# Output projection of the few-key cross-attention: one full-precision product against three rounded products

## The reference

```python
x = layernorm(x + attn(x))                       # a polynomial block and a gated feed-forward (1248 wide)
x = layernorm(x + xattn(x, ctx, mask))           # 32 heads of width 128
x = layernorm(x + ffn(x))                        # gated feed-forward (1376 wide)

# xattn
h_q, h_k, h_v = heads(rmsnorm(x) @ w_q.T), heads(ctx @ w_k.T), heads(ctx @ w_v.T)
score = softmax(where(mask, einsum('bqhd,bkhd->bhqk', h_q, h_k) + position_bias, -inf))
attn  = einsum('bhqk,bkhd->bqhd', where(mask, score, 0), h_v)
return x + attn.reshape(b, lq, 32 * 128) @ w_out.T
```

## Time and profile before

| | before |
|---|---|
| median of 3 runs | 782.0 us (781.49 to 782.08) |
| the profiled execution, its own time | 782.88 us |
| its span, first to last instruction | 781.1 us |
| PE busy | 738.4 us (95%) |
| DVE busy | 486.3 us (62%) |
| ACT busy | 402.5 us (52%) |
| POOL busy | 91.6 us (12%) |
| mean granted TensorE clock | 0.993 of full speed |
| head loop | about 223 to 640 us of the span |

### The profile page before, as it was taken

One profiled execution on the slowest core, in us unless ns is written; L12 is line 12 of the kernel. 1 busy time (PEld: TensorE's weight loads), 2 busy tenths in 40 slices (PEclk: granted clock), 3 DMA queues, 4 the chain that ended last, 5 costly groups with the idle time before them and its releaser, 6 DMA issues.

```text
span 781.1 us, 12357 instructions
## 1 busy us (share of the span) xinstructions
PE 738.4 (95%) x4320; PEld 582.0 (75%) x4320; DVE 486.3 (62%) x823; ACT 402.5 (52%) x617; POOL 91.6 (12%) x86
## 2 busy tenths in 40 slices
PE   6999999999988999999999999999999878998994
PEld 4888888888867777777777777777777547886883
DVE  5653467534352688777886586665566647578655
ACT  5433333333345666655676666766666444554452
POOL 2010000090017000000000031000000001304503
PEclk9999999999999999999999999999999999999998
DMA  9353241332625788888886777766765323542641
GB/s 331 117 219 136 84 145 54 108 122 81 241 83 179 247 300 288 265 272 290 278 277 210 227 240 232 226 222 225 245 220 175 106 96 110 155 141 84 214 133 54
DMA packets 60039, 145.09 MB, mean 186 GB/s; under 512 B 6752, under 2 KB 6768, under 8 KB 59344
## 3 DMA queue, kind: packets, MB, share of 16 engines
q1 hardware_dynamic: 58400, 136.73, 53.8%
q0 software_dynamic: 1360, 7.23, 2.4%
q10 hardware_dynamic: 224, 0.39, 0.2%
HBM read 142.23 MB, written 2.10 MB: 185 GB/s over the span
## 4 chain that ended last, share of the span: by engine, by line
PE 82%; DVE 11%; issue 2%; ACT 2%; DMA 2%; POOL 1%; DVEq 0%; ACTq 0%; POOLq 0%
PE bank L468 25%; PE acc L468 16%; PE bank L640 7%; PE bank L586 7%; PE acc L721 7%; PE bank L699 6%; PE bank L682 5%; PE bank L605 5%; DVE score L1319 2%; DVE prob L1347 1%; DVE row_sum L1341 1%; DVE piece_top L1335 1%; DVE neg_max L1325 1%; PE bank L500 1%; PE bank L666 1%
## 5 line engine op out<-in xcount | busy, mean ns | idle before, releaser
L468 PE MATMUL bank<-feat_hi,a_hi 128*128 128x512 f32 x352 | 139.3, 396 | 11.0 <-DVE feat_lo L1102 7.5
L468 PE MATMUL bank<-feat_lo,a_hi 128*128 128x512 f32 x352 | 138.0, 392 | 0.0
L1102 DVE TENSOR_TENSOR a_lo<-a_raw,a_hi 128x1024 fp32r<-128x1024 f32 (+1 forms) x45 | 55.4, 1232 | 124.3 <-ACT a_hi L867 118.0
L996 ACT ACTIVATE t_ring<-bank 128x512 f32<-128x512 f32 x64 | 70.1, 1095 | 86.3 <-PE bank L605 86.3
L586 PEld LDWEIGHTS bank<-few_ctx,ak 128*128 128x128 f32 x512 | 62.8, 193 | 45.1 <-issue 42.4
L468 PE MATMUL acc<-b_hi,tile_hi 128*128 128x512 f32 x224 | 87.7, 392 | 3.6 <-issue 1.9
L1341 DVE TENSOR_REDUCE row_sum<-prob 128x4 f32<-128x512 f32 x64 | 43.7, 683 | 71.3 <-ACT prob L1011 70.9
L468 PEld LDWEIGHTS bank<-feat_hi,a_hi 128*128 128x128 f32 x352 | 66.8, 190 | 28.0 <-DVE a_lo L1102 9.6
L468 PE MATMUL acc<-b_hi,tile_lo 128*128 128x512 f32 x224 | 87.2, 389 | 0.0
L605 PEld LDWEIGHTS bank<-k_ring,wq 128*128 128x128 f32 x512 | 64.5, 192 | 18.7 <-issue 13.4
L586 PE MATMUL bank<-few_ctx,ak 128*128 128x128 f32 x512 | 74.4, 289 | 3.4 <-DMA ak<-ax 2.1
(11 more groups left out here) (113 smaller groups left out, 1097.4 us busy)
## 6 DMA issues: line engine op xcount, KB each, us to landing
ak<-ax SPq DMA_DIRECT2D x64, 512.0 KB, 3.8
wq<-wqn SPq DMA_DIRECT2D x64, 256.0 KB, 4.2
wv<-wvh SPq DMA_DIRECT2D x64, 256.0 KB, 3.4
wo<-bx SPq DMA_DIRECT2D x64, 256.0 KB, 4.0
a_raw<-w SPq DMA_DIRECT2D x22, 512.0 KB, 4.1
a_raw<-a SPq DMA_DIRECT2D x21, 512.0 KB, 3.7
b_raw<-b SPq DMA_DIRECT2D x34, 256.0 KB, 2.7
pair<-w SPq DMA_DIRECT2D x24, 352.0 KB, 4.4
```

What stands on the lines that cost most here:

```text
L468: mm = pe.matmul(out_ap, w, x, start=start and k == 0, stop=stop and k == len(products) - 1, skip_group_check=True)
L996: act.activation(t_ring[n // GH % 2][:].rearrange("p c b k h -> p (c b k h)")[:, n % GH:GH * N:GH], bank[0][:], ACT.Copy).then_inc(t_ok, 1)
L1102: return dve.tensor_tensor(out_ap, whole, high, ALU.subtract)
```

## The change

`outer(n)` becomes three rounded products by `passes`. The operands are made as follows.

- ACT: `round_wo(n-1)` in step n, between `copy_turned` and `exponentials`, rounds the weight `wo` (128x512) into `wo_hi`. It waits for the weight's load, for the matmul that last read this `wo_hi` buffer, and for POOL's last use of it.
- POOL: `wo_rest(n)` computes `wo_lo` = `wo` - `wo_hi` (128x512), one per head. The layer norms of POOL are cut into pieces that stand between these subtractions (`normalise(1)` over heads 0 to 7, `normalise(2)` over heads 36 to 40), and the scan's `partition_all_reduce` stands behind the one of head 30.
- DVE: `split_values(n-1)` after `divide(n-1)` makes `v_hi` (a 128x128 copy) and `v_lo` (a 128x128 subtraction).
- PE: `outer(n)` waits for `v_lo_ok` and `wo_lo_ok` in place of `wo_dma`. SP's `load_o(n)` and ACT's `copy_values(n)` get one more wait each.

The new tiles lie in buffers that are free in the head loop (`tile_hi`, `tile_lo`, `b_hi`, `b_lo` of the feed-forward blocks).

```diff
+        wo_hi, wo_lo = tile_hi, tile_lo
+        v_hi, v_lo = [b_hi[i][:, 0:P] for i in range(2)], [b_lo[i][:, 0:P] for i in range(2)]
...
                 if n >= 2:
                     sp.wait_ge(out_used, n - 1)
+                    sp.wait_ge(wo_lo_ok, n - 1)
                 sp.dma_start(wo[n % 2][:], bx[n % HEADS]).then_inc(wo_dma[n % 2], 16)
...
+            def wo_rest(n):
+
+                pool.wait_ge(wo_hi_ok, n + 1)
+                pool.tensor_tensor(wo_lo[n % 2][:], wo[n % 2][:], wo_hi[n % 2][:].bitcast(F32),
+                                   ALU.subtract).then_inc(wo_lo_ok, 1)
...
             pool.wait_ge(xn_ok, C)
-            normalise(1)
-
-            pool.wait_ge(top_ok, 1)
-            pool.partition_all_reduce(piece_all[:, 1:2], piece_all[:, 0:1], P, bass.bass_isa.ReduceOp.max).then_inc(all_ok, 1)
-            pool.wait_ge(all_ok, 1)
-            pool.tensor_copy(low_flag[:], piece_all[:, 1:2]).then_inc(flag_ok, 1)
-            normalise(2)
+            scales(1)
+            for n in range(HN):
+                if n < TT:
+                    centre(1, n)
+                elif n < 2 * TT:
+                    level(1, n - TT)
+                wo_rest(n)
+                if n == GH + SCANS + 2:
+                    pool.wait_ge(top_ok, 1)
+                    pool.partition_all_reduce(piece_all[:, 1:2], piece_all[:, 0:1], P, bass.bass_isa.ReduceOp.max).then_inc(all_ok, 1)
+                    pool.wait_ge(all_ok, 1)
+                    pool.tensor_copy(low_flag[:], piece_all[:, 1:2]).then_inc(flag_ok, 1)
+                if n == HEADS + 4:
+                    scales(2)
+                if HEADS + 4 < n <= HEADS + 4 + TT:
+                    centre(2, n - HEADS - 5)
...
                     if few:
-                        pe.wait_ge(wo_dma[par], 16 * (n // 2 + 1))
-                        mm = pe.matmul(bank[1][:], v_sb[par][:, 0:P], wo[par][:], start=True, stop=True)
+                        pe.wait_ge(v_lo_ok, n + 1)
+                        pe.wait_ge(wo_lo_ok, n + 1)
+                        mm = passes(bank[1][:], v_hi[par], v_lo[par], wo_hi[par][:], wo_lo[par][:], True, True)
...
+            def round_wo(n):
+
+                act.wait_ge(wo_dma[n % 2], 16 * (n // 2 + 1))
+                if n >= 2:
+                    act.wait_ge(u_mm, n - 1)
+                    act.wait_ge(wo_lo_ok, n - 1)
+                else:
+                    act.wait_ge(b_used, T30)
+                act.activation(wo_hi[n % 2][:], wo[n % 2][:], ACT.Copy).then_inc(wo_hi_ok, 1)
...
                 if n >= 1:
                     copy_turned(n - 1)
+                    round_wo(n - 1)
                 if n >= 0:
                     exponentials(n)
...
+            def split_values(n):
+
+                dve.wait_ge(v_ok, n + 1)
+                if n >= 2:
+                    dve.wait_ge(u_mm, n - 1)
+                else:
+                    dve.wait_ge(b_used, T30)
+                dve.tensor_copy(v_hi[n % 2], v_sb[n % 2][:, 0:P]).then_inc(v_hi_ok, 1)
+                dve.wait_ge(v_hi_ok, n + 1)
+                low(v_lo[n % 2], v_sb[n % 2][:, 0:P], v_hi[n % 2].bitcast(F32)).then_inc(v_lo_ok, 1)
...
                 if n >= 1:
                     divide(n - 1)
+                    split_values(n - 1)
```

More of the change, by code:

```diff
@@ L193, in decoder_kernel @@
         poly_ok, ratio_in, ratio_ok = sem("poly_ok"), sem("ratio_in"), sem("ratio_ok")
+        wo_hi_ok, wo_lo_ok, v_hi_ok, v_lo_ok = sem("wo_hi_ok"), sem("wo_lo_ok"), sem("v_hi_ok"), sem("v_lo_ok")
         k_ok, t_ok, v_ok, u_ok = sem("k_ok"), sem("t_ok"), sem("v_ok"), sem("u_ok")
@@ L396, in scales, with centre, level @@
                 ins.then_inc(scale_ok, 1)
+            def centre(p, t):
+                if t == 0:
+                    pool.wait_ge(scale_ok, p + 1)
+                x = resid[:, (p % 2) * TT + t, :]
+                pool.tensor_scalar(x, x, moments[:, t, 0:1], scale[:, t:t + 1], ALU.subtract,
+                                   ALU.mult).then_inc(normed_ok if p < 2 else operand_ok if p < 4 else part_ok, 1)
+            def level(p, t):
+                pool.wait_ge(normed_ok, p * TT + t + 1)
+                pool.tensor_scalar(normed[:, t, :], resid[:, (p % 2) * TT + t, :], rms_scale[:, t:t + 1], None,
+                                   ALU.mult).then_inc(operand_ok, 1)
             def normalise(p):
                 scales(p)
-                pool.wait_ge(scale_ok, p + 1)
                 for t in range(TT):
-                    x = resid[:, (p % 2) * TT + t, :]
-                    ins = pool.tensor_scalar(x, x, moments[:, t, 0:1], scale[:, t:t + 1], ALU.subtract, ALU.mult)
-                    ins.then_inc(normed_ok if p < 2 else operand_ok if p < 4 else part_ok, 1)
+                    centre(p, t)
                 if p < 2:
                     for t in range(TT):
-                        pool.wait_ge(normed_ok, p * TT + t + 1)
-                        pool.tensor_scalar(normed[:, t, :], resid[:, (p % 2) * TT + t, :], rms_scale[:, t:t + 1], None,
-                                           ALU.mult).then_inc(operand_ok, 1)
+                        level(p, t)
+            def wo_rest(n):
+                pool.wait_ge(wo_hi_ok, n + 1)
+                pool.tensor_tensor(wo_lo[n % 2][:], wo[n % 2][:], wo_hi[n % 2][:].bitcast(F32),
+                                   ALU.subtract).then_inc(wo_lo_ok, 1)
             load_stage(1, xT[1])
@@ L1017, in copy_values @@
                     act.wait_ge(u_mm, n - 1)
+                    act.wait_ge(v_lo_ok, n - 1)
                 act.activation(v_sb[n % 2][:], bank[3][:], ACT.Copy).then_inc(v_ok, 1)
+            def round_wo(n):
[6 more added lines that the diff above has]
+                act.activation(wo_hi[n % 2][:], wo[n % 2][:], ACT.Copy).then_inc(wo_hi_ok, 1)
             def copy_outer(n):
@@ L1054, in step3 @@
                      f + (s0 + h * F3), last_block=True, f=f, split_next=split_next)
+            round_wo(HN - 1)
             silu(A30, s0, True, 0)
@@ L1059, in _ @@
             split_a(A30 + 1, (A30 + 1) % 2)
+            act.wait_ge(wo_lo_ok, HN)
+            act.wait_ge(v_lo_ok, HN)
             split_b(T30, T30 % 2)
@@ L1390, in _ @@
             divide(HN - 1)
+            split_values(HN - 1)
             split_a(A30 + 1, (A30 + 1) % 2)
```

## The result

The changed kernel takes 816.86 us (median of 6 runs, 815.36 to 821.99), the one before 782.16 beside it (781.49 to 785.1): ratio 1.0444, interval 1.0415 to 1.0473, or +34.7 us where +28.4 were forecast. The profiled execution took 815.36 us, its span is 813.6, against 781.1.

A forecast was written before the change was run, and what follows sets the result against it. PE was taken to bound the head loop (busy 377.65 of 388.00 us). Terms: 12.9 + 7.2 + 4.0 - 0.25 + 4 + 0.5 = +28.4 us; 782.9 + 28.4 = 811.3, less 0.9: 810 us, range 802 to 824 (60%).

The forecast's parts named there:

- the signs named: Expected profile: POOL busy near 170 us, its subtraction 1.3, `tile_hi` 0.62, plain step 5.4, gap of some 4 at head 31.
- Plain steps, 0.38 each, 12.9 in all: Steps 1 to 3 and 28 to 58, without scan: 0.53 + 0.10 - 0.25 = +0.38 us each, 12.9 us.
- the 0.10: Weight load on PE, about 0.1 us, that a matmul shows after it has waited.
- if nothing else moved: On PE, three fp32r matmuls of 0.69 us replace one of 0.94: 0.25 saved per head, 16.0 us in all.
- without that cover it costs at most 0.1: ACT's key copy, moved back by 0.6 us, stays hidden under `wo_lo`; uncovered, it costs at most 0.1 us.
- rival A: POOL is quick enough and the saving on PE shows: faster, 767 us; 6%, with another 2% for same.
- Scan steps, 7.2: Steps 4 to 27, with scan: 1.2 us per four steps, between +0.8 and +1.8; 6 x 1.2 = 7.2 us.
- the trace doesn't show: POOL's subtraction holding up the scan's masking operation on DVE: if so, another 1.0 us per four steps.
- Steps 59 to 63, 4.0; step 64: Steps that begin with the turn: 5 x 0.6 + 1.0 = 4.0 us; step 64, with its weight ready, -0.25.
- The partition reduction, 4: Between POOL's subtractions of heads 30 and 31: one preparation, 2.7 to 9.9 us, makes POOL 0 to 4.8 late; 4 taken.
- Late loads, 0.5: `load_o` waits for an earlier subtraction; a few loads land late by up to 0.5 us; 0.5 us in all.

## Why the forecast held, and where its terms were off

The direction and the mechanism were right: `outer` waits for ScalarE and POOL one behind the other, in most steps, and the time lies in the range, 7 us above the forecast. Most of these 7 us are one term, the partition reduction, taken at 4 and measured at 10. Of the signs named, POOL's subtraction (1.27 us), its busy time (174.3), `tile_hi` (0.62) and the plain step (5.39 to 5.41) came as said; PE's row shows 0.40 us of waiting ahead of the first pass, its weight load's row 0.56; the gap at head 31 was 9.0 us and not some 4.

*Plain steps, 0.38 each, 12.9 in all.* Measured 0.39 to 0.41, and 12.0 in all for 32 of the 34 steps (the other two are step 33, taken below, and step 59, which has +0.8). The first step gives 0.7, the two behind the reduction (34 and 35) give nothing, the rest 0.37 to 0.41. The parts: POOL 1.27 (taken 1.31), 0.07 and 0.14 of hand-over (0.09 and 0.06), three passes with their exposed load 0.77 (0.69 + 0.10). I put the 0.10 down to the wait. The run with 27 heads has 0.77 without any wait, so the excess over 0.69 belongs to the passes, and the saving "if nothing else moved" was 64 x 0.17 = 11 us, not 16.

*The key copy: "without that cover it costs at most 0.1".* It costs 0.17, and with passes of 0.77 us it eats the saving whole: 5.00 with the rest left out. The statement that it stays hidden under `wo_lo` was right. What it hid is that even an instant POOL would not have made plain steps faster than before, so rival A rested on a saving that the change's own order excludes.

*Scan steps, 7.2.* Measured 8.7. The split alone brings 2.3; with rounding and passes but without the rest of the weight it is 1.3; POOL's subtraction brings the other 7.4. Per four steps POOL's part is 26.45 - 25.23 = 1.22 us, half of it in the third step (6.06 with the split, 6.67 in the changed kernel). The pair that "the trace doesn't show" exists: beside POOL's subtraction the masking operation takes 1.35 to 1.62 us in place of 0.52, in 11 of 24 cases. I had taken 1.2 between +0.8 and +1.8 per four steps; 1.5 was measured, beyond the middle. The Trainium skill ("SBUF — State Buffer", "SBUF: two separate sides") says that a GpSimd operation keeps VectorE's two-port operations out for as long as it runs; the rows of this trace now agree for the integer masking, and in the run with early rounding also for the fp32r cast of 128x128 (0.22 us alone, up to 1.31 beside it).

*Steps 59 to 63, 4.0; step 64.* The turns give +4.2 for steps 59 to 64. Of this +0.8 is step 59, which belongs to the plain steps, so 3.4 stand against the 4.0; the 0.25 of the last product lies behind the last turn. The closeness may be partly luck: the granted clock is 1.00 here before the change (601.13 to 638.08), and with it 0.65 from 648.21 to 653.15 us and 0.84 from 660.78 to 671.21. How much of the 3.4 us is clock, no run separates.

*The partition reduction, 4.* This is the step of the forecast that failed: "needed: 9.9 + 0.4 + 0.3 = 10.6, so up to 4.8 us late". It counts one preparation. The trace has two, one in front and one behind, 6.46 + 7.45 us, with 0.6 between them. From the end of head 30's subtraction (452.08) to the next (466.62) that is 14.5 us against 5.8 that POOL had. PE then also loses 1.5 us to the lower clock (passes to `turn` 471.14 - 468.02 = 3.12 us, elsewhere 527.76 - 526.10 = 1.66). Measured 10.5 - 0.4 = 10.1 in the trace, 10.2 by leaving the reduction out. The 9.9 us of the earlier trace rows were not wrong as a bound on one way; the way back had no row, because before nothing that anybody waited for followed the reduction. The Trainium skill ("GPSIMD Engine Reference", "Instruction dispatch") gives about 6 us for the first call of a freshly loaded kernel. The way in agrees (6.2 us from the configuring instruction at 452.3 to 458.5). The way back, from the next configuring instruction at 459.2 to 466.6, is 7.4, and the forecast had no such price at all. That it is a loading of the same kind is inferred from the two equal instructions ahead of the two gaps; the traces show the time and no loading.

*Late loads, 0.5.* In this trace no rounding is released by its load; in the run with half of the subtraction two are, after 1.01 and 0.18 us. No run isolates them.

In sum, the medians split the time above the 781.67 us of the kernel before on that chip so: split, rounding and passes together 5.2 (of it the split alone 3.6), POOL's subtraction in the steps 19.8 (806.68 - 786.85), its switching 10.2. The 816.86 us were measured beside another run of the kernel before (782.16). By the ratios, which allow for that, the parts are 4.1, 20.7 and 9.9 us of 34.7; by their intervals each is good to some 2 or 3 us.

## What to carry to other kernels

Before an engine with slack gets a piece of a chain, write down its queue at that place: what is behind the new operation and who waits for that. The slack that decides is that of the fullest step, not the average. Here a partition reduction on POOL cost idle time in front of it and again behind it, as soon as ordinary POOL work followed that somebody waited for: count both. And a cheaper form on the bound engine pays only when all that prepares it lies in slack: the same three passes took 4.4% more here, and 0.65% less for 27 heads, with the subtraction on VectorE in place of POOL and other places in three queues.

## What the runs showed of the hardware

- POOL: 6.46 us of nothing ahead of the partition reduction and 7.45 behind it, before an ordinary subtraction (6.02 and 7.29 in the run with one f32 product).
- POOL and VectorE: beside a 1.27 us subtraction on POOL, a 128x704 int32 mask takes up to 1.62 us (else 0.52), a 128x128 cast to fp32r 1.31 (0.22), a 128x128 subtraction 1.40 (0.29), and beside two such subtractions a 128x512 operation on two SBUF inputs 1.72 (0.69). Reductions along the row kept their times (0.68 to 0.69 in all 38 that begin while it runs). Additions that read PSUM aren't settled: the two at 523.75 began before it.
- TensorE's granted clock: 0.50 behind a 9.0 us wait, 0.50 behind one of 3.17, 0.53 behind four of five waits of 1.57 us. It stayed at 1.00 behind the fifth of these, behind one of 2.04 us in the same run, and behind waits of 1.12 us in the changed kernel and 1.26 in the run with rounding early and VectorE's rest (PE's rows). What decides stays open.
- Three fp32r passes of 128x512 hold PE for 0.77 us between two groups of f32 matmuls (starts 0.30, 0.23 and 0.24 us apart at 526.10), though ten in a row start 0.23 us apart.
